# Reordering the opening of a fused attention and feed-forward kernel: VectorE's and ScalarE's order, five banks for turns and values, two wide value tiles, head 1's weights loaded earlier

## What is computed

```python
z = _layernorm(x)                                   # over the 256 columns
q, k, v = (einsum('bsd,dhk->bshk', z, W) + b for W, b in ((Wq, bq), (Wk, bk), (Wv, bv)))
attn = softmax(einsum('bqhk,bshk->bhqs', q, k) * 64 ** -0.5)
ctx = einsum('bhqs,bshk->bqhk', attn, v)
y = z + einsum('bqhk,hkd->bqd', ctx, Wo) + bo
y = (y - mean(y)) * rsqrt(var(y) + 1e-3) * gamma + beta
x = x + _layernorm(y)
x = x + _layernorm(feed_forward(_layernorm(x)))     # 256 -> 768 -> 256, gate and up
```

## Time and profile before

| | us |
|---|---|
| median of 3 runs | 2808.67 |
| the profiled execution, its own time | 2810.7 |
| its span, first to last instruction | 2808.9 |
| TensorE busy | 2698.2 (96%) |
| ScalarE busy | 2447.0 (87%) |
| VectorE busy | 2341.5 (83%) |
| GpSimd busy | 2274.6 (81%) |

### The profile page before, as it was taken

One profiled execution on the slowest core, in us unless ns is written; L12 is line 12 of the kernel. 1 busy time (PEld: TensorE's weight loads), 2 busy tenths in 40 slices (PEclk: granted clock), 3 DMA queues, 4 the chain that ended last, 5 costly groups with the idle time before them and its releaser, 6 DMA issues. The chain is left out here.

```text
span 2808.9 us, 83179 instructions
## 1 busy us (share of the span) xinstructions
PE 2698.2 (96%) x34176; PEld 1727.5 (61%) x34176; DVE 2341.5 (83%) x4203; ACT 2447.0 (87%) x4760; POOL 2274.6 (81%) x1919
## 2 busy tenths in 40 slices
PE   5899999999999999899999999999999999989997
PEld 2466666666666666556666666666666666656764
DVE  4688888999998998768888889999999998678785
ACT  3799999999999999889999999999999999846553
POOL 3799999999989999789999899999999999613232
PEclk8999999999999999999999999999999999999998
DMA  3322123212211111122221222221111122321210
GB/s 101 75 56 53 40 52 75 45 41 41 41 36 39 36 40 40 39 81 58 54 46 44 53 53 41 41 42 41 41 40 40 37 42 70 99 76 46 91 53 23
DMA packets 207100, 144.89 MB, mean 52 GB/s; under 512 B 157824, under 2 KB 181632, under 8 KB 206720
## 3 DMA queue, kind: packets, MB, share of 16 engines
q1 hardware_dynamic: 206720, 139.58, 20.6%
HBM read 51.20 MB, written 37.88 MB: 32 GB/s over the span
## 5 line engine op out<-in xcount | busy, mean ns | idle before, releaser
L536 POOL TENSOR_TENSOR p_l<-p_f,p_h 128x512 f16<-128x512 f32 x1536 | 1946.2, 1295 | 92.9 <-ACT p_h L610 90.2
L663 DVE TENSOR_REDUCE mx<-ps_aux 128x1 f32<-128x512 f32 x2048 | 1349.5, 681 | 303.9 <-PE ps_aux L834 295.8
L609 ACT ACTIVATE p_f<-ps_score 128x512 f32<-128x512 f32 x2048 | 1271.7, 622 | 18.1 <-PE ps_score L863 17.9
L610 ACT ACTIVATE p_h<-ps_score 128x512 f16<-128x512 f32 x2048 | 1280.9, 627 | 0.0
L888 PEld LDWEIGHTS ps_ctx<-v_hi_one_lo,p_h 128*128 128x128 f16 x16384 | 891.4, 97 | 245.3 <-POOL p_l L536 1.2
L888 PE MATMUL ps_ctx<-v_hi_one_lo,p_h 128*128 128x65 f16 (+1 forms) x16384 | 920.8, 193 | 1.5 <-POOL p_l L536 0.9
L888 PE MATMUL ps_ctx<-v_hi_one_lo,p_l 128*128 128x65 f16 x8192 | 791.2, 192 | 0.0
L862 PE MATMUL ps_score<-q_hilo,k_hihi 128*128 128x512 f16 x2048 | 778.2, 380 | 7.4 <-ACT v_new L568 5.4
L863 PE MATMUL ps_score<-q_hi_max,k_lo_one 65*128 65x512 f16 x2048 | 780.1, 381 | 0.0
L834 PE MATMUL ps_aux<-k_hihi,q_hilo 128*128 128x512 f16 x2048 | 620.5, 382 | 21.7 <-DVE mx L663 13.7
L681 DVE TENSOR_TENSOR p_l<-p_f,p_h 128x512 f16<-128x512 f32 x512 | 536.3, 1048 | 22.6 <-ACT p_h L610 22.6
(11 more groups left out here) (174 smaller groups left out, 2163.4 us busy)
## 6 DMA issues: line engine op xcount, KB each, us to landing
v_heads<-v_new SPq DMA_DIRECT2D x64, 258.0 KB, 2.0
v_hi_one_lo<-v_heads SPq DMA_DIRECT2D x32, 516.0 KB, 6.0
heads<-ctx_n SPq DMA_DIRECT2D x128, 128.0 KB, 2.0
x_all<-heads SPq DMA_DIRECT2D x8, 2048.0 KB, 8.7
k_hihi<-hi_st SPq DMA_DIRECT2D x62, 256.0 KB, 4.4
q_hi_max<-hi_st SPq DMA_DIRECT2D x32, 256.0 KB, 3.6
k_lo_one<-lo_st SPq DMA_DIRECT2D x32, 256.0 KB, 4.3
q_hilo<-hi_st SPq DMA_DIRECT2D x31, 256.0 KB, 3.2
```

Source lines behind the costliest of these rows:

```text
L536: nc.gpsimd.tensor_tensor(p_l[:, r], p_f[:, r], p_h[:, r], ALU.subtract).then_inc(lo_pool, 1)
L609: nc.scalar.activation(p_f[:, r], ps_score[:, bank], ACT.Exp, scale=exp_scale)
L610: nc.scalar.activation(p_h[:, r], ps_score[:, bank], ACT.Exp, scale=exp_scale).then_inc(exp_done, 1)
L663: nc.vector.reduce_max(mx[:, blk % 2, tt, ch:ch + 1], ps_aux[:, n % SIDE], AX_X).then_inc(max_read, 1)
```

## The change

Six edits, all in the opening:

- VectorE: the statistics of the second pair of groups come ahead of the split of head 0's weights; the scaling of the value weights comes behind the four `low_x` of groups 0 and 1; head 1's weights are split behind the maxima of block 0 and not behind chunk 3.
- ScalarE walks a list of its own, `act_opening_items()`: the tiles of groups 2 and 3 are scaled and `wv_h` is made ahead of chunk 0; the turns of groups 2 and 3 are taken between chunk 1 and chunk 2.
- Turns and values go round over five banks, the three of `ps_score` and the two of `ps_ctx`.
- `v_wide` has two tiles; ScalarE waits for GpSimd's value but one.
- Eight maxima come ahead of value 0; values 0 to 7 have two maxima behind them and values 8 to 15 one.
- SyncE issues the load of head 1's weights ahead of the copies of chunk 0 and not behind those of the last chunk.

```diff
         maxima = iter([(blk, kt) for blk in range(2) for kt in range(KT)])
+        order += [("max", *next(maxima)) for _ in range(KT // 2)]
         for tt in range(KT):
             order.append(("value", tt, 0))
-            order += [("max", *next(maxima)) for _ in range(2)]
+            order += [("max", *next(maxima)) for _ in range(2 if tt < KT // 2 else 1)]
...
+    def act_opening_items():
+
+        items = list(opening_items())
+        kinds = lambda kind, first, last: [i for i in items if i[0] == kind and first <= (i[1] if kind == "turn" else i[2]) <= last]
+        yield ("scale", 0, 0, 0)
+        yield from kinds("turn", 0, 1)
+        yield ("scale", 1, 0, 0)
+        yield ("wv", 0, 0, 0)
+        yield from kinds("chunk", 0, 1)
+        yield from kinds("turn", 2, 3)
+        yield from kinds("chunk", 2, 3)
+        yield from (i for i in items if i[0] == "value")
...
-        v_wide = sb("v_wide", [P, BLK], F32)
+        v_wide = sb("v_wide", [P, 2, BLK], F32)
...
+        def opening_bank(m):
+
+            return ps_score[:, m % 5] if m % 5 < RING else ps_ctx[:, m % 5 - RING]
...
                 load_w(0)
                 sp.dma_start(wv_raw, wv_src).then_inc(wv_in, 16)
                 sp.dma_start(bv_c[:, :], bv).then_inc(const_in, 16)
+                load_w(1)
                 for c in range(NB):
                     sp.wait_ge(staged, c + 2)
                     fill_high(0, slice(c * BLK, (c + 1) * BLK), high_first[c])
                 fill_low(0)
-                load_w(1)
...
-                if n:
-                    act.wait_ge(v_ready, n)
+                if n >= 2:
+                    act.wait_ge(v_ready, n - 1)
...
             def opening():
-                for kind, a, c, m in opening_items():
+                for kind, a, c, m in act_opening_items():
+                    if kind == "scale":
+                        for gr in range(2 * a, 2 * a + 2):
+                            for t in range(TB):
+                                scale_tile(0, gr, t)
+                    if kind == "wv":
+                        act.wait_ge(wv_scaled, 1)
+                        nc.scalar.activation(wv_h[:, :, :], wv_raw, ACT.Copy).then_inc(wvh_ready, 1)
...
             def opening():
                 for part in range(4):
                     norm_part(0, part)
+                for part in range(2):
+                    norm_part(1, part)
                 dve.wait_ge(const_in, 48)
                 split_w(0)
-                for part in range(4):
+                for part in range(2, 4):
                     norm_part(1, part)
-                nc.vector.tensor_scalar(bv_c[:, :], bv_c[:, :], V_SCALE, None, ALU.mult)
-                dve.wait_ge(wv_in, 16)
-                nc.vector.tensor_scalar(wv_raw, wv_raw, W_SCALE, None, ALU.mult).then_inc(wv_scaled, 1)
                 for kind, a, c, m in opening_items():
                     if kind == "turn":
-                        low_x(a * DT + c, a, c, ps_score[:, m % RING])
+                        low_x(a * DT + c, a, c, opening_bank(m))
+                        if a == 1 and c == DT - 1:
+                            dve.wait_ge(wv_in, 16)
+                            nc.vector.tensor_scalar(wv_raw, wv_raw, W_SCALE, None, ALU.mult).then_inc(wv_scaled, 1)
+                            nc.vector.tensor_scalar(bv_c[:, :], bv_c[:, :], V_SCALE, None, ALU.mult)
                     if kind == "chunk":
                         high_chunk(a, c)
-                        if c == NB - 1:
-                            split_w(1)
                     if kind == "max":
                         maximum(0, a, c, m)
                         if c == KT - 1:
                             negate(0, a)
+                            if a == 0:
+                                split_w(1)
...
             def opening():
-                free = [None] * RING
+                free = [None] * 5
```

More of the change, by code:

```diff
@@ L515, in low_value @@
                 pool.wait_ge(vh_ready, n + 1)
-                nc.gpsimd.tensor_tensor(v_new[:, n % 4, :, K + 1:VW], v_wide[:, :].rearrange("p (h k) -> p h k", k=K),
+                nc.gpsimd.tensor_tensor(v_new[:, n % 4, :, K + 1:VW], v_wide[:, n % 2].rearrange("p (h k) -> p h k", k=K),
                                         v_new[:, n % 4, :, 0:K], ALU.subtract).then_inc(v_ready, 1)
@@ L562, in take_value @@
             def take_value(n, bank):
-                if n:
-                    act.wait_ge(v_ready, n)
+                if n >= 2:
+                    act.wait_ge(v_ready, n - 1)
                 act.wait_ge(v_kept[n % 4], n // 4 * 16 + 16)
-                nc.scalar.activation(v_wide[:, :], bank, ACT.Copy, scale=V_SCALE / X_SCALE / W_SCALE)
+                nc.scalar.activation(v_wide[:, n % 2], bank, ACT.Copy, scale=V_SCALE / X_SCALE / W_SCALE)
                 nc.scalar.activation(v_new[:, n % 4, :, 0:K], bank.rearrange("p (h k) -> p h k", k=K), ACT.Copy,
@@ L586, in opening @@
             def opening():
-                for kind, a, c, m in opening_items():
+                for kind, a, c, m in act_opening_items():
[6 more added lines that the diff above has]
+                        nc.scalar.activation(wv_h[:, :, :], wv_raw, ACT.Copy).then_inc(wvh_ready, 1)
                     if kind == "turn":
[L589 to L592, removed]
                         act.wait_ge(pro_full, m + 1)
[L594 to L597, removed]
+                        take_turned(a, c, opening_bank(m))
                     if kind == "chunk":
@@ L601, in opening @@
                         act.wait_ge(pro_full, m + 1)
-                        take_value(a, ps_score[:, m % RING])
+                        take_value(a, opening_bank(m))
             def head(g, u, maxima, items):
@@ L905, in opening @@
                     if kind == "turn":
-                        turn_x(a, c, ps_score[:, m % RING], pro_full)
+                        turn_x(a, c, opening_bank(m), pro_full)
                         free.append((x_split, a * DT + c + 1))
                     if kind == "value":
-                        value(a, ps_score[:, m % RING], pro_full)
+                        value(a, opening_bank(m), pro_full)
                         free.append((vh_ready, a + 1))
```

## The result

The changed kernel takes 2787.12 us (median of 4 runs, 2786.54 to 2788.39) against 2808.79 us (4 runs, 2808.62 to 2809.34): 21.7 us less, a ratio of 0.9922 with a 95% interval of 0.9906 to 0.9938. The direction was as forecast, and so was the mechanism inside the opening; the size was not, and part of the gain lies where the forecast had ruled one out. The forecast was 2790.8 and its range ended at 2787.5, 0.4 us above what was measured.

What follows compares the result with a forecast made beforehand. TensorE was taken to set the end from the first weighing on. Value 0 at 39.7 plus 25.8, 0.3, 2.1, 2.30 and 8.03 put that weighing at 78.2 against 96.09: 2808.67 - 17.9 = 2790.8 us, range 2787.5 to 2795.5.

Steps and rivals of the forecast that it cites:

- the change touches no step behind it: Everything behind the first weighing stays as long as before, so the gain is that moment's shift, 17.9 us.
- the low clock at value 0: TensorE, lightly loaded from 33 to 39 us, starts the values at the low clock: 2.1 us lost, between 0 and 3.1.
- the tail: From GpSimd's end of the last value to the first weighing: 8.03 us as before, its stores and load unchanged.
- VectorE and ScalarE up to chunk 0: Opening's reordered work: second shift done at 18.44 us, chunk 0 taken by ScalarE at 24.8 against 25.59.
- Chunks 1 to 3: ScalarE takes chunk 1 from 27.28 us, chunk 2 at about 32.0 and chunk 3 at 35.1; all staged at 37.5.
- rows 8 show a stretched cast, not one that waits out a neighbour: Profile's head casts, 408 to 783 ns beside GpSimd, were read as slowed: chunk 2's cast takes 0 to 0.4 us more.
- Eight maxima: Ahead of the values, VectorE paces the maxima at 0.62 us each from 36.2 us; value 0 starts at 39.7.
- A: Rival: TensorE's clock falls between 69 and 78 us, so the first weighing starts low; 2793.7 us, chance 0.20.
- B: Rival: the second tile doesn't remove the wait, values stay 2.38 us apart; shift 9.0, 2799.7 us, chance 0.05.
- C: Rival: more is won, clock up at value 0 and chunk 2 taken at the high clock; 2788.0 us, chance 0.09.
- D: Rival: slower, the clock stays low for all of the values; 2813.6 us, chance 0.02.
- E: Rival: the shift is given back in head 0; 2808.7 us, chance 0.02.

Runs made afterwards that it cites:

- one_wide_in_heads: The changed kernel with one wide tile again for the values made inside the heads, two kept in the opening: 2789.60 us, ratio 0.9929 to the kernel before.
- three_banks: The changed kernel with turns and values over the three banks of `ps_score` again instead of five: 2790.16 us, ratio 0.9932 to the kernel before.
- after_again: The changed kernel itself, unaltered, run again in a later group: 2787.40 us, ratio 0.9920 to the kernel before.
- one_wide_in_opening: The changed kernel with one wide tile in the opening and two in the heads: 2798.29 us, ratio 0.9961 to the kernel before.
- values_first_mended: The changed kernel without maxima ahead of value 0, four stores issued ahead of the low halves' copies, head 1's weights split behind block 1: 2780.69 us.
- before_two_wide_heads: The kernel before, with two wide tiles for values made inside the heads and one in the opening: 2807.21 us, ratio 0.9993.
- all_of_it: `values_first_mended` with the load of head 0's values in two halves and scores started bank by bank: 2780.74 us, ratio 0.9898 to the kernel before.

## Why the prediction missed

The step that put the time outside the range is "the change touches no step behind it" (and with it "Six edits, all in the opening"): the second tile also shortens head 15, by 1.65 us. Without these 1.65 us the median would be 2788.8, and `one_wide_in_heads`, which is the change without them, measured 2789.60; both lie inside the range. Two more terms were mis-sized the same way: the low clock at value 0 (2.1 against 0.6 us) and the tail (8.03 against 6.98).

Point by point, in the profile's time (forecast, then measured):

- **VectorE and ScalarE up to chunk 0**: right, 24.8 and 24.16. The take of the fourth turn was estimated to end at 18.85 and ended at 18.54. (Three `low_x` from 18.44 end at 20.32 and not 20.35; nothing hangs on it.)
- **Chunks 1 to 3**: 35.1 and 34.58, the 0.6 carried over from chunk 0. The cast beside `wv_l` took 1.05 us more and not 0 to 0.4. Here the step "rows 8 show a stretched cast, not one that waits out a neighbour" is false. Beside `wv_l` the cast waited until it ended, and rows 8 held the same wait: in the trace of before, 16 of their 30 casts met a GpSimd instruction, and each ended 0.28 or 0.29 us behind it. The 783 ns are those of casts that began 0.5 us ahead of such an end. The misreading cost the 0.2 us that the prediction had worked out for this case and no more, since low half 2 stood behind `wv_l` anyway. By the Trainium skill, GPSIMD Engine Reference, section Key points, the two engines share their ports into SBUF; the trace agrees, and adds that a cast ends 0.27 to 0.29 us behind the GpSimd instruction that it met: in ten executions the cast beside `wv_l` or a piece of it began at different times and took 0.57 to 1.86 us, and every one ended so. In `three_banks` it began 0.11 us ahead of the end and took its usual 0.43. A cast slowed in proportion could not do that.
- **Eight maxima**: right in kind. VectorE's eight took 4.87 us, TensorE's value 0 started at 39.24 (39.7), 0.5 early by the terms above.
- **The low clock at value 0**: mis-sized, 2.1 against 0.6. I let it start with value 0, as after the long wait of the earlier trace rows. It had fallen before, at 37.0, in the stretch of the maxima, and was up 1.2 us into the values. It also differs between executions of one kernel: in `after_again` the values lost nothing. Over the profiles with eight maxima ahead of value 0 and the tile and weights as changed the loss was 0 to 1.4 us.
- **The rest of the values**: 25.8 us as computed, and 0.32 us of wait for VectorE's split at 50.27 (0.3).
- **The tail**: 8.03 carried over from the earlier trace rows, 6.98 measured. The step "that tail holds stores and a load which the change leaves as they are" is true of the instructions and not of the time: the load, from its issue to the weighing that waits for it, took 4.84 to 5.10 us in eight profiles and 5.9 to 6.2 in three, two of these the only two with the opening of before. `three_banks` had 6.01 with the same instructions behind the last value as the changed kernel. I took one execution's value for a constant. Nor is the load all of the tail's path any more: TensorE's scores and the chunk behind them, from 67.53 to 75.13, end with it in the changed kernel, and in `one_wide_in_opening` and `values_first_mended` the weighing follows them without a wait. A faster load alone would have won next to nothing.
- **"The change touches no step behind it"**: false, and the largest single error. `take_value` and its tile serve the heads too. In head 15 sixteen values are made, close together, and two tiles are worth 1.65 us there: TensorE no longer waits for a bank that ScalarE empties late. `one_wide_in_heads` and `before_two_wide_heads` show it from both sides.

The sum: value 0 0.5, clock 1.5, tail 1.05 and 0.1 less in small terms put the first weighing at 75.3 instead of 78.2, 2.9 us. The first query block gives 0.4 back, head 15 adds 1.65, the rest of the span 0.2: 17.9 + 2.9 - 0.4 + 1.65 + 0.2 = 22.3, the span's difference.

Of the rivals, A (a second low clock from 69 to 78 us) did not come: the granted clock stayed at 1.00 there and through the heads. B was tested by its own mechanism and is worth 11.5 us. C named the clock, which was one of the sources, and chunk 2 at the high clock, which came (it was taken at 31.11) but won nothing, since its low half stood queued behind `wv_l`. With both it still ended at 2788.0. D and E fell with the first profile.

The range was too narrow for a reason that can be named: its lower end was made of clock terms alone, and none of my cases held a gain outside the opening or a faster tail.

Not settled: why the load takes about 5 us in most executions and 5.9 to 6.2 in some. In the half microsecond from 5.0 us behind its issue, the three slow ones still move 8 to 15 GB/s, and seven of the others nothing. Whether the old opening makes the slow case more frequent can't be told from two profiles of it. No run changed that load alone.

## What to carry to other kernels

When a change edits a helper or the depth of a buffer, list every caller before writing that the rest is untouched; a tile that is too shallow in one stage is mostly too shallow wherever the same loop runs densely. A stretch in which the engine that sets the end keeps another one's pace (here TensorE at VectorE's maxima) is worth a reordering, but look at once for what the earlier work will meet: the queue of stores, and the helper engine's casts beside a busy GpSimd. Take DMA durations and clock stretches from several executions, and give each of them both ends in the range. And before reading a spread of durations as a slowdown, set each instruction beside its neighbour's end: a wait shows as a common distance from it.

## What the hardware showed

- A VectorE cast from float32 to float16 in SBUF does not run slowly beside a GpSimd subtraction, it waits: 0.57 to 1.86 us in eight executions beside one subtraction of 4.07 us (1.48 in the changed kernel, 1.86 in `all_of_it`), 1.00 against the last of four pieces, 0.43 where GpSimd was idle. Each of these that was delayed ended 0.27 to 0.29 us behind the GpSimd instruction. A long GpSimd instruction is a long stall for whoever needs such a cast.
- TensorE's clock fell to the lower level, at 37.0 us in the changed kernel, while TensorE was not idle but lightly used: four matmuls since 33.4, with no pause above 1.35 us. With the same four matmuls it stayed up in `after_again`.
- One and the same load of 516 KB took 4.7 to 5.1 us from issue to landing in ten executions and 5.8 to 6.1 us in three.
